# Three layers of attention and mixing on one core: twelve stack transfers for sixteen, masks first in every second unit, low halves of queries and keys made by TensorE and ScalarE, and a new order of turns

## The reference, cut to what matters

```
x = x + L0_attn(layernorm(x))          # 16 heads of 32, causal, biases on q, k, v and out
x = x + L0_xattn(layernorm(x), ctx)    # 32 query heads of 16 over 8 key heads ("mix")
x = x + L0_ffn(layernorm(x))           # weights and activations rounded to blocks of 32
x = x + L1_attn(layernorm(x))          # state scan over 256 steps ("ssm")
x = x + L1_xattn(layernorm(x), ctx)    # 16 heads of 32, causal ("cross")
x = x + L1_ffn(layernorm(x))           # eight low-rank experts, two of them chosen ("lora")

# L0_attn (L1_xattn is alike, without biases and with keys and values from ctx)
q = x @ Wq.T + bq;  k = x @ Wk.T + bk;  v = x @ Wv.T + bv
attn = softmax(where(j > i, -1e9, q @ k.T / sqrt(32)))
out = (attn @ v) @ Wo.T + bo
```

## Time and profile before

| what | value |
|---|---|
| median of three runs | 1706.04 us |
| the profiled execution's own time | 1713.42 us |
| its span on the core | 1711.4 us |
| mean granted clock of TensorE | 0.905 of full |
| TensorE, VectorE, ScalarE, GpSimd busy | 1421.5, 1383.0, 1018.4, 425.6 us |

### The profile page before, as it was taken

One profiled execution on the slowest core, in us unless ns is written; L12 is line 12 of the kernel. 1 busy time (PEld: TensorE's weight loads), 2 busy tenths in 40 slices (PEclk: granted clock), 3 DMA queues, 4 the chain that ended last, 5 costly groups with the idle time before them and its releaser, 6 DMA issues.

```text
span 1711.4 us, 30964 instructions
## 1 busy us (share of the span) xinstructions
PE 1421.5 (83%) x11920; PEld 734.5 (43%) x11920; DVE 1383.0 (81%) x2111; ACT 1018.4 (60%) x1852; POOL 425.6 (25%) x486
## 2 busy tenths in 40 slices
PE   0877768778898899898987876689989999999986
PEld 0444424335345354435434333344555555555542
DVE  4988878969969788887779699987688979888743
ACT  2234237265474573746476577887689877879531
POOL 1351114032241241322221232222123222131310
PEclk9777869879899899999799999979999999999998
DMA  6214031120210202001130000320120202011020
GB/s 215 65 47 111 1 94 38 32 63 13 45 38 15 57 20 54 23 8 35 42 116 24 16 25 1 102 53 9 41 59 2 66 2 66 1 42 41 2 75 25
DMA packets 92080, 76.37 MB, mean 45 GB/s; under 512 B 9376, under 2 KB 73888, under 8 KB 91424
## 3 DMA queue, kind: packets, MB, share of 16 engines
q1 hardware_dynamic: 91936, 74.40, 16.0%
HBM read 39.24 MB, written 9.44 MB: 28 GB/s over the span
## 4 chain that ended last, share of the span: by engine, by line
PE 43%; DVE 29%; ACT 10%; issue 8%; SPq 5%; POOL 3%; DMA 2%; ACTq 0%; DVEq 0%; POOLq 0%
PE bank L194 14%; DVE mix_NM L1035 6%; PE bank L1135 3%; PE bank L503 3%; SPq L704 3%; PE bank L511 2%; PE bank L491 2%; PE bank L948 2%; DVE ssm_HS L1495 2%; PE bank L463 2%; PE bank L933 2%; DVE ffn_m L1089 1%; DVE ffn_Z L1099 1%; PE bank L1161 1%; PE bank L526 1%
## 5 line engine op out<-in xcount | busy, mean ns | idle before, releaser
L1008 ACT ACTIVATE mix_P<-bank 128x512 f32<-128x512 f32 x256 | 141.8, 601 | 61.4 <-PE bank L933 60.0
L1035 DVE TENSOR_REDUCE mix_NM<-bank 128x2 f32<-128x512 f32 x256 | 164.5, 683 | 11.5 <-PE bank L908 11.4
L1495 DVE TENSOR_TENSOR_SCAN ssm_HS<-ssm_DA,ssm_DD 128x1024 f32<-128x1024 f32 x64 | 151.5, 2368 | 13.5 <-ACT ssm_DD L1446 7.4
L1253 POOL TENSOR_TENSOR ffn_room<-ffn_room 128x512 f32<-128x512 f32 x64 | 90.0, 1407 | 275.8 <-ACT ffn_room L1192 168.9
L687 POOL TENSOR_SCALAR_AFFINE_SELECT attn_P<-attn_P 128x256 f32<-128x256 f32 x128 | 87.7, 696 | 285.1 <-ACT attn_P L595 284.8
L687 POOL TENSOR_SCALAR_AFFINE_SELECT cross_P<-cross_P 128x256 f32<-128x256 f32 x128 | 87.9, 696 | 281.7 <-ACT cross_P L595 281.7
L595 ACT ACTIVATE attn_P<-bank 128x384 f32<-128x384 f32 x128 | 63.6, 497 | 89.0 <-PE bank L492 88.6
L1443 ACT ACTIVATE ssm_DA<-ssm_Z,A_T 128x255 f32<-128x255 f32 x256 | 111.8, 498 | 4.0 <-DVE ssm_HS L1495 3.5
L595 ACT ACTIVATE cross_P<-bank 128x384 f32<-128x384 f32 x128 | 62.7, 490 | 47.9 <-PE bank L492 47.5
L1135 PE MATMUL bank<-gate,ffn_XQ 128*128 128x512 bf16 x256 | 74.0, 416 | 14.5 <-DVE ffn_room L1217 13.7
L1501 DVE TENSOR_TENSOR ssm_HS<-ssm_HS,ssm_CS 128x1024 f32<-128x1024 f32 x64 | 81.7, 1276 | 1.0
(11 more groups left out here) (403 smaller groups left out, 4121.9 us busy)
## 6 DMA issues: line engine op xcount, KB each, us to landing
attn_stack<-attn_P SPq DMA_DIRECT2D x64, 128.0 KB, 2.5
cross_stack<-cross_P SPq DMA_DIRECT2D x64, 128.0 KB, 2.5
ffn_room<-f_gate SPq DMA_DIRECT2D x4, 1024.0 KB, 5.3
XR<-x SPq DMA_DIRECT2D x8, 512.0 KB, 6.4
attn_stack<-attn_P SPq DMA_DIRECT2D x64, 64.0 KB, 2.2
ffn_room<-f_up SPq DMA_DIRECT2D x4, 1024.0 KB, 5.2
ffn_room<-f_down SPq DMA_DIRECT2D x4, 1024.0 KB, 5.5
x_mid<-XR SPq DMA_DIRECT2D x8, 512.0 KB, 3.4
```

What stands on the lines that cost most here:

```text
L1008: nc.scalar.activation(self.p[h % 8], bank[b4[h % 2]][:, :], ACT.Exp, scale=HD2 ** -0.5).then_inc(s["p_ready"], 1)
L1035: nc.vector.tensor_reduce(self.nm[:, t, 16 * i + 2 * g:16 * i + 2 * g + 2], bank[b4[u % 3]][:, :].rearrange("p (c k) -> p c k", c=2), AX.X ...
L1253: nc.gpsimd.tensor_tensor(self.inter[q % 2][:, 512 * (g % 2):512 * (g % 2) + 512], self.sg[g % 2], self.up[g % 2], ALU.mult).then_inc(s["i ...
L1495: nc.vector.tensor_tensor_scan(flat(self.hs), flat(self.da), flat(self.dd), 0.0, ALU.mult, ALU.add).then_inc(s["hs_ready"], 1)
```

## The change

1. **Stack.** `qk` now has the parts in the order high q, low q, high k, low k. Head h lies at place 4j + c of the stack, so that one transfer writes four heads in one run. Twelve transfers of 128 KB per sample take the place of 16 (eight of 64 KB and eight of 128 KB); the bytes are the same.
2. **Masks by turns.** In odd units the mask comes first and the scores after it. In the odd ones of the last eight units the scores are four matmuls of 128 columns and no longer two of 256.
3. **Joined casts.** In `cross`, one cast and one subtraction of 512 columns take the place of two each of 256 columns.
4. **Low parts in attn.** TensorE multiplies the high parts by a negative identity into the bank that still holds q and k, and ScalarE reads the rest, adds the bias and writes the low part. VectorE's L627 is gone. Two constants more are made at the start.
5. **Loaders.** `weights_f` follows `weights_a`, which follows `weights_0`; each waits for the one before.
6. **Turns.** All five tables are new; `attn` has two steps more per sample on TensorE and ScalarE (and four fewer on VectorE).

```diff
-        Q_LOW, K_HIGH, Q_HIGH, K_LOW = range(4)
+        Q_HIGH, Q_LOW, K_HIGH, K_LOW = range(4)
@@ Loader.sp
+                if i == 0 and self.before is not None:
+                    sp.wait_ge(*self.before.ready())
@@ Attention.pe
-                for c in range(DC):
+                for c in range(DC + 2):
+                    if c >= 2 and self.bq is not None:
+                        yield
+                        pe.wait_ge(self.qh_ready, DC * n + c - 1)
+                        nc.tensor.matmul(bank[self.b[c % 3]][:, :].rearrange("p (i k) -> p i k", i=2), negative[:],
+                                         self.qk[:, Q_HIGH:K_LOW:2, c - 2, :], start=False, stop=True,
+                                         skip_group_check=True).then_inc(self.ql_ps, 1)
+                    if c >= DC:
+                        continue
...
+                    masked = u % 2 == 1
+                    for part in ("mask", "scores") if masked else ("scores", "mask"):
...
@@ Attention.act
+                for c in range(DC + 2):
+                    if c >= 2 and self.bq is not None:
+                        yield
+                        act.wait_ge(self.ql_ps, DC * n + c - 1)
+                        for i, part, bias in ((0, Q_LOW, self.bq), (1, K_LOW, self.bk)):
+                            last = nc.scalar.activation(self.qk[:, part, c - 2, :], bank[self.b[c % 3]][:, i * S:(i + 1) * S],
+                                                        ACT.Identity, bias=bias[:, c - 2:c - 1])
+                        last.then_inc(self.qk_ready, 1)
...
+                    if self.bq is None:
+                        last = nc.scalar.copy(self.qk[:, Q_HIGH:K_LOW:2, c, :],
+                                              bank[self.b[(2 + c) % 3]][:, :].rearrange("p (i k) -> p i k", i=2))
@@ Attention.dve
-                for c in range(DC):
+                for c in range(DC if self.bq is None else 0):
...
+                    nc.vector.tensor_tensor(self.qk[:, Q_LOW:K_LOW + 1:2, c, :], src,
+                                            self.qk[:, Q_HIGH:K_LOW:2, c, :], ALU.subtract).then_inc(self.qk_ready, 1)
@@ Attention.sp
-                    for slot, i, parts in ((0, slice(0, 1), slice(Q_HIGH, Q_HIGH + 1)),
-                                           (0, slice(1, 2), slice(K_HIGH, K_HIGH + 1)),
-                                           (1, slice(0, 2), slice(Q_LOW, K_HIGH + 1)),
-                                           (2, slice(0, 2), slice(Q_HIGH, K_LOW + 1))):
-                        sp.dma_start(dst[32 * slot:32 * slot + 32, i], self.qk[rows, parts]
+                    for slot, parts in enumerate((slice(Q_HIGH, K_LOW, 2), slice(Q_LOW, K_LOW), slice(Q_HIGH, K_LOW + 1, 3))):
+                        sp.dma_start(self.stack[32 * slot:32 * slot + 32, :, 4 * j:4 * j + 4, :], self.qk[rows, parts]
                                      ).then_inc(self.stack_in, 16)
@@ TURNS0, first line of SyncE's table
-        "eekalkkaacakkebbeeeccbbaecebcbeecccbcebeccbccbdaccdaccbbccdacbcbccccccbdbdcfjmmmfmmcmccdfcdfndnn"
+        "ekakcekalkkaabebeeaccbebeebccbececebcbeccccbcbdaccbcdacbccdacbbcccccdccbbcdmffmmcjmmmccdcfnnnddf"
```

More of the change, by code:

```diff
@@ L215, in make_constants @@
             own(nc.gpsimd.memset(identh[:], 0.0))
+            own(nc.gpsimd.memset(negative[:], 0.0))
             own(nc.gpsimd.memset(hide_qk[:], 0.0))
@@ L227, in make_constants @@
                                             pattern=[[-1, P]], channel_multiplier=1))
+            own(nc.gpsimd.affine_select(out=negative[:], in_=negative[:], compare_op=ALU.not_equal, fill=-1.0, base=0,
+                                        pattern=[[-1, P]], channel_multiplier=1))
             own(nc.gpsimd.affine_select(out=hide_qk[:], in_=hide_qk[:], compare_op=ALU.is_ge, fill=MASKED,
@@ L243, in __init__ @@
                     self.loaded, self.high_ready, self.low_ready = before.loaded, before.high_ready, before.low_ready
-                self.first = 0 if before is None else len(before.items)
-                self.used = [0 if before is None else len(range(i, len(before.items), len(stage))) for i in range(len(stage))]
+                self.before = before
+                self.first = 0 if before is None else before.first + len(before.items)
+                self.used = [0 if before is None else before.used[i] + len(range(i, len(before.items), len(stage)))
+                             for i in range(len(stage))]
             def ready(self, count=None):
@@ new lines, in pe @@
+                    for part in ("mask", "scores") if masked else ("scores", "mask"):
+                        begins, ends = part == ("mask" if masked else "scores"), part == ("scores" if masked else "mask")
+                        if part == "mask" and u < 4:
+                            last = nc.tensor.matmul(bank[b][:, :].rearrange("p (c k) -> p c k", c=DC), ident16[:],
+                                                    broadcast(hide_qk[:, :], 1, DC), start=begins, stop=ends)
+                        elif part == "mask":
+                            last = nc.tensor.matmul(
+                                bank[b][:, :].rearrange("p (c k) -> p c k", c=2)[:, :, P:S], ident16[:],
+                                broadcast(hide_qk[:, :], 1, 2), start=begins, stop=ends)
+                        elif u < 4:
+                            for c in range(DC):
+                                last = nc.tensor.matmul(bank[b][:, c * P:(c + 1) * P], q[:, c, 0:P], k[:, c, 0:P],
+                                                        start=(begins and c == 0), stop=(ends and c == DC - 1))
+                        else:
+                            for i in range(2):
+                                c = 2 * ((u - 4) // 4) + i
+                                for keys in (slice(0, P), slice(P, S)) if masked else (slice(0, S),):
+                                    last = nc.tensor.matmul(bank[b][:, i * S + keys.start:i * S + keys.stop], q[:, c, P:S],
+                                                            k[:, c, keys], start=(begins and i == 0),
+                                                            stop=(ends and i == 1 and keys.stop == S))
@@ L1301, in pe @@
                 if n == 0:
-                    pe.wait_ge(weights_a.low_ready, len(weights_a.items))
+                    pe.wait_ge(*weights_a.ready())
                 banks.take(b)
```

175 lines of the change are left out of this document (76 added, 99 removed).

## The result

The changed kernel took 1618.22 us (median of four runs, 1616.83 to 1621.32). Its ratio to the kernel before is 0.9479, with a 95% interval of 0.9458 to 0.9500: 88 us or 5.2% less. Beside the kernels of two later groups it gave 0.9481 and 0.9490. I had forecast 1676, at best 1655. The direction was right, and the size was missed by 58 us.

The account below looks back on a forecast made before the run. No engine alone was taken as the bound, but a late start and then a chain of waits across engines. Terms of -40.5 us, reduced to -30.5 for sharing, gave 1676 us after scaling to the median; range 1655 to 1699.

Parts of the forecast that it names:

- Start, -10.5: At the program's start, the context lands earlier, so ScalarE's first cast begins earlier: -10.5 us, between -4 and -16.
- Four transfers fewer, -6: Stack issue on SyncE: four fewer issues per sample shorten the chain by 6 us, between 0 and -12.
- Stack ahead of mix's maxima, -6: Third and fourth samples' stacks issued before mix's transfers gain 5 and 3 us, fifth loses 2: -6, between -15 and +6.
- Low parts, -10: First-layer attention: moving low parts off VectorE gains 16 and 4 us, less added costs: -10, between -20 and +16.
- The +10 that I set against it: Costs of moving low parts: +5 us for the longer end of q and k, +5 for TensorE's 32 matmuls.
- Masks, -6: Cross attention's scores and masks: fewer changes between 32 and 128 rows on TensorE save 6 us, between 0 and -15.
- The 0.86 us for two units: Expected sign in cross: two units take TensorE 0.86 us at full clock where VectorE allows.
- rival of scores running beside each other: Masks: 71 pairs of neighbouring scores of two row groups overlap on TensorE, beside the full sum: 1655 us, chance 0.05.
- Joined casts, -2: Cross: joining VectorE's casts, and the same on ScalarE, saves 2 us.
- I keep two thirds: Whole kernel: the five terms besides the start hide behind each other on one chain, so their 30 us become 20.
- rival of the full sum: Whole kernel: terms add without sharing, since engines at 88% leave little cover: -40.5 us, 1666 us, chance 0.12.
- TensorE at its new waits: First layer: TensorE stops 32 times for ScalarE's casts of high parts, making the kernel slower, about 1725 us; chance 0.07.

Follow-up runs that it names:

- turns_oldsp: Kernel before with the new order on TensorE, VectorE, ScalarE and GpSimd and SyncE's new first 13 turns, then SyncE's old order; no edits; ratio 0.9754.
- before_newstart: Kernel before with only the first 13 turns of SyncE's table exchanged for the changed kernel's; ratio 0.9912.
- after_dummy: Changed kernel with 64 more VectorE instructions where the low parts stood, for which nobody waits; ratio 0.9592 to the kernel before.
- undo_low: Changed kernel with the low parts of q and k back on VectorE, without the negative identity and ScalarE's low parts; ratio 0.9591 to the kernel before.
- turns_only: Kernel before with the new order of turns in all tables and none of the edits; ratio 0.9703.
- edits_old_turns: Changed kernel with the old order of turns, adjusted only as the low parts need; ratio 0.9910 to the kernel before.

## Why the prediction was right or wrong

**The step that failed** is the inventory of the change: "six" turned every table, and I priced of it the start and two moved stacks, "Together -6". The remaining tables had no term. They are worth 27 us (turns_oldsp less the start), and the order as a whole raises the edits from 15 to 38 us. After my cut by a third I had 10.5 us for the start, 4 for the stacks and 16 for the edits. Measured are 15, 11 for all of SyncE's turns behind the start, 38 for the edits in the new order, and the 27 that had no term: 5, 7, 22 and 27 us more, which is the miss of 58 us within the intervals. The trace of the kernel before had a hint: VectorE's two largest waits, 35.6 and 31.8 us, and 328 us of idle time beside 290 of TensorE's. No rival of mine reached below 1655.

**Start, -10.5.** The mechanism and its times were right: the cast at 13.31 for 13.5. With the new start alone (before_newstart) the first cast of q began at 38.70 for the forecast 39.2, 11.0 us earlier than before. The other tables moved it on to 36.52, and TensorE's first product from 32.41 to 24.55 (forecast 27). Measured -15, within -4 to -16; with an interval of 5 us the 10.5 is not excluded.

**Four transfers fewer, -6.** Measured -14. I took half of a quarter of 46 us of chain rows, mostly of the first 600 us. There the issues turned out hidden in the new order. The gain came behind 750 us, where of the last 411 us the rows had only 9 us: the new order put 30 there. So the wrong size follows from the step that failed: rows of the old order were used for an edit in a new one. One reading was also off. The time from 228.13 to 237.99 spans 15 intervals and not 16, since the last issue begins as its transfer does. That is 0.66 us each.

**Stack ahead of mix's maxima, -6.** The mechanism was right and the size too small. The first score came 8.0 us earlier at the third sample, of at most 8.9. I halved that because TensorE had mix's work to do, but TensorE stood idle for 10 us ahead of that score, so no half was due. The fourth sample added 9.5 where I had 3, and the fifth took back 3 where I had 2. All of SyncE's turns behind the start give -11 at the end; the two stacks were not tried alone.

**Low parts, -10.** The relief of VectorE was sized right for the new order: -16 - 4 = -20 against 19 measured. For the old order it was not measured alone; all edits together gave 15 there. The +10 that I set against it, for the longer end of q and k and for TensorE's 32 matmuls, is not there: after_dummy and undo_low are level.

**Masks, -6.** Measured -7, give or take 6. The changes between 32 and 128 rows as the cause were argued and not shown. The 0.86 us for two units was not seen: in the second layer VectorE's maxima run at 0.62 us each (4.34 over seven), as they did before in such a run (3.10 over five), and TensorE follows them:

```profile
1112.92 0.77 PE L487 MATMUL bank<-cross_P 32*128 32x128 f16 x6
1113.16 4.34 DVE L669 TENSOR_REDUCE cross_NM<-bank 128x2 f32<-128x512 f32 x7
```

So the rival of scores running beside each other, from the Trainium skill's TensorEngine Tiling (Array Packing), Key Properties, stays undecided: at VectorE's pace these rows can't show it.

**Joined casts, -2.** Not tried alone. The edits other than the low parts give 19 us together (turns_only to undo_low), stack and masks 21, so little is left for them.

**"I keep two thirds."** No run shows this loss. In the old order start and edits give 24 for 30, which is within the intervals. In the new order the low parts, the stack and the masks taken back one at a time cost 19 + 14 + 7 = 40, against 38 for all edits together. They add, as far as the intervals tell, which is what my rival of the full sum had.

**TensorE at its new waits.** Refuted, 0.2 us on average. The rival's sum was also wrong: 1706 - 40.5 + 62 is 1727.5, and with a third of the gains not reached it would be some 1741 and not 1725.

## What to carry to other kernels

When a change brings new tables of turns, the order is a term of its own, and the worth of the other edits depends on it: work taken off an engine turned into idle time until the turns around it moved, and issues that one order hid stood on the chain in another. Read the engines' largest waits and their total idle time as what a new order may return (here 60 of 328 us on VectorE), and let the range reach there. To learn what an edit's relief is worth, give the engine the same work back as instructions for which nobody waits.

## What the runs showed of the hardware

Six issues from ScalarE held it for 4.04 us, 0.67 each, as long as SyncE needs (8.10 for twelve). With two queues at work the stack's transfers of the second layer landed in 4.2 to 4.3 us in place of 2.5 (KB each, median us from issue to landing):

```profile
cross_stack<-cross_P SPq DMA_DIRECT2D x48, 128.0 KB, 4.3
cross_stack<-cross_P ACTq DMA_DIRECT2D x48, 128.0 KB, 4.2
```

From these rows I estimate 8.0 us from the first issue of a stack to its last landing with two queues (the last issue begins 3.8 us after the first), and 9.9 with one (7.4 + 2.5). The Trainium skill's page DMA: Bandwidth & Descriptors says in "Issuing engines are not separate DMA queues" that issuing from several engines saves only the time on the sequencer that issues, which is usually small beside the transfer. The first half agrees with the slower landing. The second holds here for one transfer (0.67 us beside 2.4) and not for a stack, whose landings overlap: eleven issues make up 7.4 of its 9.9 us.

TensorE's mean granted clock, at a busy share of 83% before and 85% after, rose with the change. It was 0.905 of full in the profiled execution of before, but 0.903 to 0.918, 0.911 on average, in the 49 executions of before beside the experiments. In 14 executions of the changed kernel it was 0.936 on average, in four of edits_old_turns, with the same instructions and some 76 us more, 0.922. With 160 more matmuls recorded TensorE's busy time fell by 47 us. Among the executions of one kernel, before or changed, a clock lower by 0.01 goes with some 10 us more. If that held between the kernels too, the clock's 0.025 would make 25 of the 88 us; this is an estimate, and the runs do not separate the clock from the order that leaves TensorE less idle. The 19 us of after_dummy are not of this kind: its clock was 0.935.
